# Two layers of attention on one core: the order of each slot is rearranged, with inputs transposed a slot sooner

## What is computed

```python
xn = layernorm(x, g_in)
q = (xn @ Wq).reshape(b, n, H, DH).transpose(0, 2, 1, 3)   # layer 0: times DH ** -0.5
kv = xn @ Wkv                                              # layer 1: q and k l2-normalised
sim = einsum('bhid,bjd->bhij', q, k) + bias                # causal and key mask
attn = softmax(sim)
out = einsum('bhij,bjd->bhid', attn, v)
x = x + layernorm(out @ Wo, g_out)
```

## Time and profile before

| | us |
|---|---|
| median of 3 runs | 2150.11 |
| lowest, highest run | 2148.06, 2150.55 |
| the profiled execution's own time | 2145.81 |
| its span, first to last instruction | 2144.0 |
| TensorE busy | 2078.9 |
| VectorE, ScalarE, GpSimd busy | 1600.9, 1554.9, 1028.4 |
| mean granted TensorE clock | 0.99 of 2.4 GHz |

### The profile page before, as it was taken

How to read it: one execution, slowest core, us unless ns; L and a number is a source line. 1 busy time by engine, 2 the same in 40 slices (tenths; PEclk the granted TensorE clock), 3 DMA queues, 4 the chain that set the end, 5 groups by cost and what they waited for, 6 DMA issues and landing times.

```text
span 2144.0 us, 72068 instructions
## 1 busy us (share of the span) xinstructions
PE 2078.9 (97%) x26363; PEld 1857.0 (87%) x26363; DVE 1600.9 (75%) x3422; ACT 1554.9 (73%) x6241; POOL 1028.4 (48%) x1510
## 2 busy tenths in 40 slices
PE   5899999999999999999999999999999999999987
PEld 4788988988988988988988988988988888988876
DVE  4877777777777777777777777777777777777765
...
DMA packets 183034, 147.47 MB, mean 69 GB/s; under 512 B 121440, under 2 KB 125616, under 8 KB 182992
## 3 DMA queue, kind: packets, MB, share of 16 engines
...
...
## 4 chain that ended last, share of the span: by engine, by line
PE 92%; ACT 2%; DVE 2%; SPq 2%; POOL 1%; issue 1%; DMA 1%; POOLq 0%; DVEq 0%; ACTq 0%
PE psum L708 32%; PE psum L614 18%; PE psum L580 16%; PE psum L691 9%; PE psum L673 8%; PE psum L542 3%; PE psum L631 3%; PE psum L591 2%; ACT o_hi L908 1%; SPq L386 1%; ACT probs L902 1%; POOL probs L1479 1%; DMA k_high<-kv_t 1%; POOL masked_bias L1469 0%; PE psum L622 0%
## 5 line engine op out<-in xcount | busy, mean ns | idle before, releaser
L902 ACT ACTIVATE probs<-probs,neg_max 128x129 f32<-128x129 f32 (+3 forms) x2048 | 712.5, 351 | 56.2 <-DVE neg_max L1144 56.0
L1469 POOL TENSOR_TENSOR masked_bias<-bias,pad_neg 128x516 f32<-128x516 f32 (+3 forms) x512 | 395.9, 806 | 213.9 <-DVE probs L1138 208.2
L1479 POOL TENSOR_TENSOR probs<-probs,den_inv 128x512 f32<-128x512 f32 (+3 forms) x512 | 371.5, 747 | 146.9 <-DVE den_inv L1149 146.9
L1491 POOL TENSOR_TENSOR y_out<-y_out,res 128x512 f32<-128x512 f32 x128 | 165.4, 1292 | 526.8 <-ACT y_out L866 526.8
L902 ACT ACTIVATION_READ_ACCUMULATOR probs<-probs,neg_max 128x1 f32 x2048 | 386.0, 188 | 0.0
L1154 DVE STREAM_TRANSPOSE probs_t<-probs 128x512 f32<-128x512 f32 (+3 forms) x512 | 230.0, 487 | 195.9 <-POOL probs L1479 194.8
L1138 DVE TENSOR_TENSOR probs<-psum,masked_bias 128x648 f32<-128x648 f32 x256 | 212.8, 832 | 113.7 <-PE psum L673 110.8
L708 PE MATMUL psum<-wo_hi,o_hi 128*128 128x512 f32 x1024 | 271.6, 407 | 7.9 <-ACT o_hi L908 7.5
L908 ACT ACTIVATE o_hi<-psum,null_v_col 128x512 fp32r<-128x512 f32 x256 | 162.0, 683 | 157.1 <-PE psum L691 157.1
L708 PE MATMUL psum<-wo_hi,o_lo 128*128 128x512 f32 x1024 | 262.5, 398 | 0.0
L708 PE MATMUL psum<-wo_lo,o_hi 128*128 128x512 f32 x1024 | 260.7, 396 | 0.0
...
## 6 DMA issues: line engine op xcount, KB each, us to landing
...
v_rep<-v_kept SPq DMA_DIRECT2D x512, 32.0 KB, 1.8
...
```

What stands on the lines that cost most here:

```text
L902: x_ = nc.scalar.activation(s, s, ACT.Exp, bias=neg_max[:, b, n:n + 1], accum_out=den[:, b, n:n + 1])
L1469: m = nc.gpsimd.tensor_tensor(block(masked_bias, b), block(bias[u.layer], b), pad_neg[u.layer][:, 0:WIDTH[b]].unsqueeze(1).to_broadcast([P ...
L1479: m = nc.gpsimd.tensor_tensor(some, some, den_inv[:, b, :].unsqueeze(2).to_broadcast([P, 4, n]), ALU.mult)
```

## The change

Every slot of TensorE gets one order: input projection, output projection, then both score groups of the next unit and the values of this one in one piece (`score_values`). Both adds of the bias stand together at the end of VectorE's slot (`add_biases`), in `late` with group 1 first. An input tile is transposed one slot before it is projected: layer 1's tiles in `first` and `second`, a pair's two tiles in the second `late` (`ready` is one whose normalised form is there already, `fresh` one that is normalised in the slot, `kept` one that is only normalised in it). In `late` the last part of the output projection comes right before the scores. The squares and inverse roots of layer 1 on ScalarE come earlier among the exponentials. The tile q_t is now a view of q_sb, and x_hi, x_lo get space of their own. At the start, the DMAs of the upper keys and of q_aside go from SyncE's queue to ScalarE's, ahead of the loads of the output weights, and the loads of the key masks stand ahead of the bias loads. In `second` the wait for `pair_v_ready` now stands ahead of the scores.

```diff
-    second0(A(1), A(0), pair(1), B(0), A(2))
-    late0(A(2), A(1), B(0), A(4), (A(4), A(5)), B(0), 2)
+    second0(A(1), A(0), pair(1), B(0), A(2), None)
+    late0(A(2), A(1), B(0), (), (A(4), A(5)), None, (A(4), A(5), B(1)), B(0))
     with eng.Fori(2, nb // 2 - 1) as j:
         four = {k: eng.snap(j * 4 + k) for k in range(-9, 6)}
...
         w = Pair(one[0], a(0), a(1), two[1], two[2])
         first(b(-4), a(-2), w, b(-3), a(-1))
-        late(a(-1), b(-4), b(-3), None, (b(-2),), b(-3), 0)
-        second(b(-3), a(-1), w, b(-2), a(0))
-        late(a(0), b(-3), b(-2), a(2), (a(2), a(3)), b(-2), one[1])
+        late(a(-1), b(-4), b(-3), (), (), b(-2), (b(-2),), b(-3))
+        second(b(-3), a(-1), w, b(-2), a(0), a(2))
+        late(a(0), b(-3), b(-2), (a(2),), (a(3),), None, (a(3), b(-1)), b(-2))
     m = nb - 2
...
-
-        q_t = sb("q_t", [P, 2, BLOCKS, P])
+        x_hi = sb("x_hi", [P, D], F32R)
+        x_lo = sb("x_lo", [P, D], F32R)
+
         q_sb = sb("q_sb", [P, INNER])
...
                 load_pieces(sp, range(KC))
                 start(sp, rows_loads[:3], rows_loaded[0])
+                for k in range(2):
+                    sp.dma_start(keep[k][:, :], row((keep0, keep1)[k][0], S)).then_inc(keep_loaded[k], 16)
                 load_xa(n)
                 start(sp, rest_loads, rest_loaded)
-                for k in range(2):
-                    sp.dma_start(keep[k][:, :], row((keep0, keep1)[k][0], S)).then_inc(keep_loaded[k], 16)
                 start(sp, rows_loads[3:], rows_loaded[1])
                 start(sp, [(null_v[:, :], row(null_kv[1], DH))], null_v_loaded)
                 load_res(w.even)
-                put_aside(w)
-                copy_keys(w)
                 start(sp, g_out_loads, g_out_loaded)
...
-                load_keep_behind(then)
-
+                run_stages((load_keep_behind, then), (part(finish, u), v))
+
+            def second(u, v, w, n, then, n2):
+                run_stages((load_xa, n2), (load_keep_behind, then))
                 wait_apart(sp, scores_done[0], u.done, sp_passed)
                 put_aside(w)
                 run_stages((copy_keys, w), (part(copy_pair_v, v if u.layer else u), w), (part(finish, u), v))

-            def late(u, v, w, n, loads, then, pairs_done):
+            def late(u, v, w, ready, fresh, kept, loads, then):
                 run_stages((load_xa, loads[0] if loads else None), (load_keep_behind, then), (part(copy_unit_v, v), w),
-                           (load_xa, loads[1] if len(loads) > 1 else None), (part(finish, u), v))
+                           (load_xa, loads[1] if len(loads) > 1 else None), (part(finish, u), v),
+                           (load_xa, loads[2] if len(loads) > 2 else None))
...
-            def transpose_even(w, u):
+            def transpose_input(x, u):
                 if u:
                     wait(pe, biased[0], u.done)
-                transpose_x(w.even)
-
-            def transpose_odd(w):
-                wait(pe, x_lo_done, w.odd.xprev)
-                transpose_x(w.odd)
-
-            def transpose_second(w, u):
-                wait(pe, biased[0], u.done)
-                transpose_x(w)
+                wait(pe, x_lo_done, x.xprev)
+                transpose_x(x)
...
+            def score_values(then, order, u):
+                if then:
+                    for c in order:
+                        scores(then, c)
+                if u:
+                    values(u, range(BLOCKS))
...
             def first(u, v, w, n, then):
-                scores(u, 1)
-                transpose_even(w, u)
+                project_pair(w, 0, (0, 1), u)
                 project_out(v, 0, u)
                 project_out(v, 1)
-                transpose_odd(w)
+                transpose_input(n, u)
                 project_out(v, 2)
-                project_pair(w, 0, (0, 1, 2, 3), u)
-                scores(then, 0)
-                values(u, range(BLOCKS))
-
-            def second(u, v, w, n, then):
-                scores(u, 1)
+                project_pair(w, 0, (2, 3), u)
+                wait(pe, x_lo_done, n.xdone)
+                score_values(then, (0, 1), u)
+
+            def second(u, v, w, n, then, n2):
+                project_pair(w, 1, (0, 1), u)
+                wait(pe, o_lo_done[0], v.done)
+                project_kv(w)
                 project_out(v, 0, u)
                 project_out(v, 1)
+                transpose_input(n, u)
                 project_out(v, 2)
-                project_kv(w)
-                project_pair(w, 1, (0, 1, 2), u)
+                project_pair(w, 1, (2,), u)
                 transpose_v(w)
                 project_pair(w, 1, (3,), u)
-                scores(then, 0)
                 wait(pe, pair_v_ready, w.pdone * 2)
-                values(u, range(BLOCKS))
-
-            def late(u, v, w, n, loads, then, pairs_done):
-                if u:
-                    scores(u, 1)
-                if w:
-                    transpose_second(w, u)
-                project_out(v, 0, u)
+                wait(pe, x_lo_done, n.xdone)
+                score_values(then, (0, 1), u)
+
+            def late(u, v, w, ready, fresh, kept, loads, then):
                 if w:
                     project(w, u, v)
+                for x in ready:
+                    transpose_input(x, u)
+                project_out(v, 0, u)
                 project_out(v, 1)
-                project_out(v, 2)
+                for x in fresh[:-1]:
+                    transpose_input(x, u)
                 if w:
                     transpose_k(w)
                     transpose_q(w)
+                for x in fresh[-1:]:
+                    transpose_input(x, u)
+                project_out(v, 2)
+                if w:
                     wait(pe, keys_ready, w.sdone)
-                if u:
-                    if not w:
-                        wait(pe, o_lo_done[0], u.prev)
-                    values(u, range(2))
-                if then:
-                    scores(then, 0)
-                if u:
-                    values(u, range(2, BLOCKS))
+                elif u:
+                    wait(pe, o_lo_done[0], u.prev)
+                for x in (ready + fresh)[-1:]:
+                    wait(pe, x_lo_done, x.xdone)
+                score_values(then, (1, 0), u)
...
+                null_norm()
+                for k in range(2):
+                    wait(act, half_copied[k], w.first)
+                act.dma_start(q_aside[:, :, :], qp[:, 0, BLOCKS:2 * BLOCKS, :]).then_inc(aside_loaded, 16)
+                wait(act, kvt_ready, w.pdone)
+                act.dma_start(k_high[DH:P, :, :], kv_t[0:DH, :, :]).then_inc(k_high_loaded, 16)
                 load_pieces(act, range(KC, 2 * KC))
...
+            def late(u, v, w, ready, fresh, kept, loads, then):
                 if u:
                     exponential(u, 0)
                 if w:
                     square(w, 0)
+                    square(w, 2)
                 if u:
-                    exponential(u, 1)
+                    exponential(u, 1, (2,))
                 if w:
-                    square(w, 2)
+                    square(w, 1)
                     inverse_root(w, 0)
-                    square(w, 1)
+                for x in ready:
+                    split_x(x)
+                if w:
                     inverse_root(w, 2)
-                if n:
-                    rstd_of_input(n)
-                if w:
                     inverse_root(w, 1)
-                take_y(v)
+                if u:
+                    exponential(u, 1, (0,))
+                for x in fresh[:-1]:
+                    rstd_of_input(x)
+                    split_x(x)
+                if kept:
+                    rstd_of_input(kept)
+                for x in fresh[-1:]:
+                    rstd_of_input(x)
                 if w:
                     take_qt(w)
+                for x in fresh[-1:]:
+                    split_x(x)
+                take_y(v)
                 rstd_of_output(v)
+                scale_output(v)
                 if u:
                     split_o(u)
-                scale_output(v)
...
-            def add_bias(u, c):
-                if c == 0:
-                    for g in range(len(GROUPS)):
-                        wait(dve, turned[g], u.prev)
-                    wait(dve, masked_bias_done, u.done)
-                wait(dve, scores_done[c], u.done)
-                nc.vector.tensor_tensor(pairs(probs, c), SB[c][:, :, 0:ROW], pairs(masked_bias, c), ALU.add).then_inc(biased[c], 1)
+            def add_biases(u, order):
+                for g in range(len(GROUPS)):
+                    wait(dve, turned[g], u.prev)
+                wait(dve, masked_bias_done, u.done)
+                for c in order:
+                    wait(dve, scores_done[c], u.done)
+                    nc.vector.tensor_tensor(pairs(probs, c), SB[c][:, :, 0:ROW], pairs(masked_bias, c), ALU.add).then_inc(biased[c], 1)
...
```

(88 more changed lines are left out.)

193 lines of the change are left out of this document (85 added, 108 removed).

## The result

The changed kernel takes 2285.05 us (median of 4 runs, 2284.01 to 2286.74) against 2149.47 for the kernel before (also four runs). The ratio is 1.063, 95% interval 1.062 to 1.065: slower by 136 us. I forecast slower, 2218 us, with a range up to 2250; the direction was right, the size was not.

A forecast was written before the change was run, and what follows sets the result against it. TensorE's chain of pieces was taken as the bound. New waits of 3.0 us a turn against 0.75 saved gave 65 us over 29 turns; 2145.8 + 65 + 2 + 1 = 2213.8, plus 4.3 to the median: 2218 us, range 2153 to 2250.

The forecast's parts named there:

- The bound: In the loop, TensorE's pieces laid end to end sum to 63.82 us a turn, 0.75 less than before.
- Step 1: End of each `late`: the next slot's projection waits for VectorE's add, a stall of 0.6 us twice a turn.
- Step 2: In `second`, before the scores: TensorE waits for the pair's v, a stall of 0.6 us a turn.
- Step 3: In the second `late`: transposes of the fresh input wait for xn, a stall of 1.1 us a turn.
- Step 4: End of `first`: VectorE's second add ends at 14.7 against TensorE's end at 14.70, a stall of 0.1 us.
- Rival C: In the loop, gaps drop TensorE to its lower clock, 2.2 us a turn more, 2282 us; chance 0.03.
- Rival A: In the loop, the new waits don't bite and only the 0.75 us saving remains, 2123 us; chance 0.14.
- B: Only the stalls at the end of `late` bite, +0.45 us a turn, 2166 us; chance 0.18.
- Queues: SyncE's moved loads stay hidden, GpSimd's idle time covers its wait for both adds, q^T in q's place costs nothing.
- The start: Before the loop: keys' DMA saves 4 us, `second0` costs 1, `late0` costs 5 (0 to 8); +2 us together.

The follow-up runs named there:

- e1: The changed kernel with ScalarE's copy of the pair projection's second half moved ahead of the output's root and scaling in `first`: 2223.14 us.
- e14: e1 with VectorE adding both groups' biases ahead of the output's centring in `late`: 2282.70 us.
- e12: e1 with, in `second`, TensorE's wait for v between scores and values and ScalarE's last half copied before the output's root: 2202.94 us.
- e16: e12 with VectorE taking the fresh input's statistics ahead of `den_inv` in the `late` that transposes it: 2186.99 us.
- e7: The changed kernel with ScalarE's copy in `first` held back until the slot's output is stored, widening the gap: 2470.24 us.
- e17: e14 with ScalarE making `o_hi` before the output's root and scaling at the end of `late`: 2280.91 us.
- e5: The changed kernel with four edits: early copy in `first`, later v wait in `second`, group 1's add before centring, fresh input's statistics and root earlier: 2239.37 us.
- e8: The kernel before with only q^T kept in q's place and x_hi, x_lo given their own memory: 2147.01 us.
- e10: The kernel before with only the DMAs of upper keys and set-aside queries moved to ScalarE's queue, ahead of its weight loads: 2141.79 us.
- e15: The kernel with e16's edits and e14's adds, plus the first layer-1 input normalised ahead of the weights' low parts in `second0`: 2242.75 us.

## Why the prediction was right in direction and wrong in size

**The bound.** TensorE's pieces end to end, 29 turns, and no slack: right. e1's `first`, freed of its gap, takes 14.80 us (326.42 to 341.22), against 14.70 of pieces and 0.1 of stall. That e1's whole turn, 66.80, is my 66.8 is luck: my three kinds of stall measure about 2.55 us instead of 2.9, the 0.1 isn't seen, and the pieces take some 0.4 more than 63.82.

**Step 1, the end of `late`: mechanism right, size somewhat too large.** The wait for the add was to be 0.6 twice; it is 0.30 and 0.21 at the projection's first matmul (14.8 us over 58 times), and some 0.2 more lies inside the scores, 1.70 instead of 1.50 (330.71 to 332.41), which I take for group 0's wait for the copy of y. In sum 0.4 to 0.5 each, against 0.6. What I hadn't seen is that this price is well spent: taking it away cost three times as much (e14).

**Step 2, v in `second`: right.** 0.6 forecast; the row says 0.79 (22.9 in 29 times), and e12 shows 0.62 of it on the path.

**Step 3, xn in the second `late`: right.** 1.1 forecast, 0.87 measured; it is VectorE's statistics behind `den_inv`, and e16 halves the wait and gets 0.59 a turn back by that order alone.

**Step 4, the end of `first`: the step that failed.** I put VectorE's adds against TensorE's end there, found 14.7 against 14.70, and called it 0.1. I didn't follow the other thing for which a score group waits, the copy of the banks it is written into. The change sets group 1 right behind the projection that fills those banks, so `half_copied` became a wait with nothing beside it (for the scores the section on the kernel before names `y_taken` alone); and the diff of ScalarE's `first` shows the copy as its last step but one, behind an output root whose input I had myself placed late, behind VectorE's transposes. The price is 1.74 a turn, 50 us, and with it the clock. In `second` I did list the pieces in the same way and missed the same copy there; I take it to lie under the wait for v, since e12 moved both at once and no run has it alone.

**Rival C, the clock: dismissed too early.** I gave it 0.03 because my gaps were 1.1 at most. The gap that I had missed was long enough: four falls in 29 turns, 6 us, and by my estimate another 7 in the start, for which I had no clock at all. C's number, 2282, is 3 us from the measured one by luck: it charged 2.2 us to each turn, and the clock took 0.22. The rule of the Trainium skill (TensorE: Matmul & The Clock Gate, HAM oscillation), that a loop with waits between bursts can send each burst back to the slow clock, holds here in e7, where it does so in every turn; in the changed kernel it does so in one turn of seven, and in the loop behind gaps of 0.9 to 1.5 us (e1, e17, e5) in none.

**Rival A and B.** The new waits did bite, all of them, so A fell; B left out steps 2 and 3, which e12 and e16 show at 0.6 each.

**Queues.** GpSimd's wait for both adds and SyncE's moved loads appear in no wait of TensorE in the loop, as argued. q^T in q's place costs nothing (e8), as argued.

**The start: mis-sized.** +2 forecast, +14.8 measured. The part with the keys' DMA was right at its place (4.7 sooner at the first transposes, 46.09 against 50.78, where I took 4; alone it is worth 5 to 11 at the end, e10). What I took as 1 us in `second0`, the first output that has to be finished inside the slot, is the 5.27 us wait for xn, and 1.45 for x_lo behind it: the reason was right and the size wrong, since that way runs through the output's centring, scaling and GpSimd's addition, with 1.35 for the low parts that VectorE has ahead of it (e15); what I took as 5 in `late0` is 2.06 and 3.06 for its two fresh inputs, within my 0 to 8, but the low parts of weights now also end last, 4.29 against 3.10 before. About 7 us are the clock. I had priced each edit of the start by the loop's rows, in which VectorE has no weights to split and the granted clock is 1.00.

**The sum mended.** 2218 as forecast, + 29 x 1.98 (68.78 less 66.8) = 57, + 13 for the start, gives 2288, against 2285 measured. It closes because it puts in what was measured; the step that failed and its dips are 57 of the 70 us. That the mended loop (e16, 65.58) still stands above the kernel before (64.57), although its pieces sum to 63.82, is the ends of the two `late` slots and what is left of the wait for xn: 1.76 us, of which 0.43, 0.29 and 0.22 are waits in its trace and twice 0.2 lie in the scores; for the last 0.4 I have no row.
